# A mamba layer with a routed mixture of experts on one core: first fold, tag loads, an early turn and a reshared combine

## What is computed

```python
# layer 1: mamba-like block, then an MLP (256 -> 1024 -> 256)
xn = layernorm(x) * w + b
g = xn @ gate_w + gate_b                      # halves gate, gate_gate through silu
u  = (xn * gate) @ state_w + state_b
Bm = gate_gate @ state_w + state_b
delta = softplus(mean(xn @ state_w + state_b))
y = scan(h = exp(-delta) * h + delta * Bm * u)
x = x + y @ out_w + out_b
x = x + gelu(layernorm(x) @ mlp_w1 + mlp_b1) @ mlp_w2 + mlp_b2
# layer 2: 8 experts, 2 chosen for each token
xn = layernorm(x) * ln_gamma + ln_beta
abel_out = gelu(xn @ abel_w + abel_b)
topw, topi = top_k(xn @ moe_gate_w + moe_gate_b, 2); w = softmax(topw)
eo[e] = gelu(xn @ ew1[e] + eb1[e]) @ ew2[e] + eb2[e]
moe_out = sum_e w[e] * eo[e];  moe_out = moe_out @ expm(gens[i])  for i in 0..2
gate = sigmoid(concat(abel_out, moe_out) @ gc_w + gc_b)
out = layernorm(x + residual + abel_out * (1 - gate) + moe_out * gate)
```

## Time and profile before

| what | value |
|---|---|
| time of three runs | 727.7, 729.74, 888.66 us, median 729.74 |
| the profiled execution | 730.6 us, of which 728.7 us from the first to the last instruction |
| PE / PEld / DVE / ACT / POOL busy | 87% / 65% / 81% / 64% / 34% |
| mean granted TensorE clock | 0.945 |
| DMA | 99.21 MB, mean 136 GB/s |

### The profile page before, as it was taken

How to read it: one execution, slowest core, us unless ns; L and a number is a source line. 1 busy time by engine, 2 the same in 40 slices (tenths; PEclk the granted TensorE clock), 3 DMA queues, 4 the chain that set the end, 5 groups by cost and what they waited for, 6 DMA issues and landing times. The chain is left out here.

```text
span 728.7 us, 16183 instructions
## 1 busy us (share of the span) xinstructions
PE 632.1 (87%) x4525; PEld 473.6 (65%) x4526; DVE 587.5 (81%) x1535; ACT 462.9 (64%) x876; POOL 248.2 (34%) x295
## 2 busy tenths in 40 slices
PE   6899999999999999999979995889999999996000
PEld 5667557575665857566556884678888888885000
DVE  4989768899998999899798875577788878784693
ACT  4346573956658494765757344667777777774197
POOL 2111020125436081633516540133434344444042
PEclk9999999999999999999998997999999999999555
DMA  5643223165644537356725824465666655310974
GB/s 146 197 148 58 87 42 80 55 127 193 117 152 103 135 109 157 119 103 236 171 87 176 275 99 109 112 162 148 160 166 160 164 132 126 77 58 4 303 246 144
DMA packets 124502, 99.21 MB, mean 136 GB/s; under 512 B 60432, under 2 KB 114587, under 8 KB 124316
## 3 DMA queue, kind: packets, MB, share of 16 engines
q1 hardware_dynamic: 108028, 68.82, 33.4%
q0 software_dynamic: 16416, 29.67, 17.4%
HBM read 62.42 MB, written 33.68 MB: 132 GB/s over the span
## 5 line engine op out<-in xcount | busy, mean ns | idle before, releaser
L1920 POOL DMA_INDIRECT scratch_ys<-ye,place x78 | 86.9, 1114 | 149.4 <-ACT ye L1964 109.5
L79 PE MATMUL up<-shared,words 128*128 128x256 bf16 x936 | 112.3, 278 | 13.0 <-PEq L1738 7.8
L79 PE MATMUL bank<-words 128*128 128x512 bf16 (+1 forms) x576 | 109.4, 343 | 3.8 <-DVE logits L1077 3.2
L79 PE MATMUL down<-words,shared 128*128 x936 | 110.5, 274 | 1.8 <-DVE yb L2051 1.1
L79 PEld LDWEIGHTS up<-shared,words 128*128 x936 | 93.1, 100 | 26.9 <-issue 14.3
L79 PEld LDWEIGHTS down<-words,shared 128*128 128x128 bf16 x936 | 90.8, 98 | 15.9 <-issue 3.6
L79 PE MATMUL bank<-xn_s,mlp_w 128*128 128x512 bf16 x384 | 89.5, 387 | 2.2 <-DVE xn_s L798 2.2
L79 PEld LDWEIGHTS bank<-words 128*128 128x128 bf16 x576 | 55.4, 98 | 50.4 <-issue 6.6
L79 PE MATMUL bank<-mlp_w,shared 128*128 128x256 bf16 x768 | 86.4, 273 | 0.0
L510 POOL DMA_INDIRECT scratch_zs<-rows,pos x64 | 71.0, 1109 | 37.2 <-DVE pos L1127 18.5
L79 PEld LDWEIGHTS bank<-mlp_w,shared 128*128 128x128 bf16 x768 | 74.9, 98 | 10.6 <-issue 0.4
(11 more groups left out here) (247 smaller groups left out, 1151.4 us busy)
## 6 DMA issues: line engine op xcount, KB each, us to landing
fetched<-scratch_zs SPq DMA_DIRECT2D x156, 64.0 KB
words<-scratch_ys SPq DMA_DIRECT2D x16, 514.0 KB, 8.5
scratch_abel<-staged SPq DMA_DIRECT2D x8, 514.0 KB, 3.7
abel_all<-scratch_abel SPq DMA_DIRECT2D x8, 514.0 KB
x_in<-in_x SPq DMA_DIRECT2D x8, 512.0 KB, 5.6
words<-in_out_b_row SPq DMA_DIRECT2D x8, 512.0 KB, 4.1
fetched<-in_mlp_b_row SPq DMA_DIRECT2D x8, 512.0 KB, 3.5
words<-in_x POOLq DMA_DIRECT2D x8, 512.0 KB, 7.9
```

The lines of the kernel that those rows point to most:

```text
L79: last = nc.tensor.matmul(dst, lhs(a, k), rhs(b, k), start=start and n == 0, stop=stop and n == total - 1)
L1920: nc.gpsimd.indirect_dma_start(out=ys_dram[:, :], out_offset=bass.IndirectOffsetOnAxis(ap=place[:, k, s:s + 1], axis=0), in_=ye[:, k % 2, ...
```

## The change

Line numbers below are those of the diff; none of the arithmetic that is wanted changes, but for the order of the additions' engines.

1. **First fold and ring.** The ring's order becomes ew1 0 to 3, ew2t 0, ew1 4 to 7, ew2t 1 to 7. `fold(0)` runs around `turn2(LAST)`, its heads and tails in that region; all later folds, heads and tails move up by one expert, and one `w1_tails` moves from before the last routing but one to behind it. `fold_bank` and the waits of chunks 0 to 7 follow.
2. **Nine products** `ident` x `turnmat` that nobody reads, behind the last fold (`BUSY_BEFORE_TILES`).
3. **Tile 1 turned early**, in phase 1 instead of in `body(0)`; ScalarE's table load moves to phase 1 too; all `w2_heads` and `w2_tails` come ahead of the turn of tile 0.
4. **Tag loads one by one**: each `load(q)` issues the tags of its own tile; tiles 0 and 1 follow in `load(2)` and `load(3)`. `load_branch` comes behind a group's four loads.
5. **Half steps at the bias**: `down` signals each of its two halves, `biased` waits for each.
6. **The combine** is shared out anew (last part of the diff): TensorE adds the two rows of a token (identity times `got`, two float32 products of 257 columns for each token tile, into PSUM) for half of batches 1 and 2 and for all of 3 to 7; VectorE then only subtracts; batch 0 is loaded and added in halves; 30 unread products (`KEPT_BUSY`) run ahead of the sums; of the four finishing operations ScalarE keeps two, GpSimd does two in batches 0 to 5 and VectorE two in batches 6 and 7. The orders on VectorE and ScalarE follow.

```diff
+        RAW_ORDER = [("ew1", e) for e in range(RAW - 1)] + [("ew2t", 0)] \
+            + [("ew1", e) for e in range(RAW - 1, NE)] + [("ew2t", e) for e in range(1, NE)]
...
-            return bank[(0, 1, 5, 4)[m % 4] if m < 4 * FC else (6, 7, 0, 1, 5, 4)[(m - 4 * FC) % 6]]
+            return bank[(2, 0, 1, 4)[m] if m < 4 else (0, 1, 5, 4)[m % 4] if m < 4 * FC else (6, 7, 0, 1, 5, 4)[(m - 4 * FC) % 6]]
...
             norm2_split(LAST)
+            w2_tails((0,))
             norm3_rows(LAST - 1)
...
             z4_tails(LAST - 1)
-            w1_tails((4,))
+            w2_tails((1, 2, 3))
             gelu_tail(LAST, 4)
             gelu_tail(LAST, 5)
-            w1_tails((5,))
+            w1_tails((4,))
...
-            w1_tails((6,))
+            w1_tails((5, 6))
             branch_sum(LAST, LAST % 2, 0)
             w1_tails((7,))
             branch_sum(LAST, LAST % 2, 1)
             norm3(LAST)
-            w2_tails(range(0, FC))
+            w2_tails(range(FC, 2 * FC))
...
-            dve.wait_ge(zs_in[0], 64)
-            turn_rows(nc, xt[:, 0], xb[:, 0], xT_done)
-            w2_tails(range(NE * FC - 3, NE * FC - 1))
+            for n in range(FETCHED):
+                dve.wait_ge(zs_in[n], 64)
+                turn_rows(nc, xt[:, n], xb[:, n], xT_done)
...
+            fold(0, (0, 1))
             turn2(LAST)
+            fold(0, (2, 3))
             mlp_up(LAST, range(0, 2))
+            pe.wait_ge(w2_tail, 1)
             turn4(LAST - 1, BATCHES)
             mlp_up(LAST, range(2, HC))
+            pe.wait_ge(w2_tail, FC)
             branch(LAST - 1, BATCHES)
             mlp_down(LAST, (0,))
             ranks(LAST - 1)
             mlp_down(LAST, (1,))
-            fold(0)
             fold(1)
+            fold(2)
             turn4(LAST, BATCHES + 1)
-            fold(2, (0, 1))
+            fold(3, (0, 1))
             branch(LAST, BATCHES + 1)
...
+            pe.wait_ge(w2_tail, 6 * FC)
+            for n in range(BUSY_BEFORE_TILES):
+                nc.tensor.matmul(bank[2 + n % 2][:, 0:DG], ident[:, :], turnmat[:, n % KC], start=True, stop=True)
...
 +                else:
+                    dve.wait_ge(sum_r, summed(b))
+                    nc.vector.tensor_tensor(diff[:, b % 2], banks[:, b % 2 * TT:b % 2 * TT + TT, 0:DG], abel[:, b],
+                                            ALU.subtract).then_inc(diff_r, 1)
...
+            def finished(b):
+                pool.wait_ge(shift_r, b + 1)
+                for n in pool_tiles(b):
+                    nc.gpsimd.tensor_scalar(got[:, b, 0, n, 0:D], mix[:, b % MIX, n], rs[:, b % 2, n:n + 1],
+                                            shift[:, b % 2, n:n + 1], ALU.mult, ALU.add).then_inc(res_p, 1)
...
             differ(0)
+            mixed(0)
             differ(1)
-            mixed(0)
-            for b in range(BATCHES):
-                if b + 2 < BATCHES:
-                    differ(b + 2)
-                if b > 0:
+            variances(0)
+            mixed(1)
+            shifts(0)
+            finished(0)
+            differ(2)
+            for b in range(1, BATCHES):
+                if b > 1:
                     shifts(b - 1)
+                    finished(b - 1)
                 if b + 1 < BATCHES:
                     mixed(b + 1)
                 variances(b)
+                if b + 2 < BATCHES:
+                    differ(b + 2)
...
+            def sums(b):
+                if b > 2:
+                    pe.wait_ge(diff_r, differences(b - 2))
+                pe.wait_ge(got_in[b], 32)
+                for n in range(added_by_vector(b), TT):
+                    nc.tensor.matmul(banks[:, b % 2 * TT + n, 0:DG], ident[:, :], got[:, b, 0, n], start=True, stop=False)
+                    nc.tensor.matmul(banks[:, b % 2 * TT + n, 0:DG], ident[:, :], got[:, b, 1, n], start=False, stop=True)\
+                        .then_inc(sum_r, 1)
...
+            pe.wait_ge(yb_r, ST * QT)
+            for n in range(KEPT_BUSY):
+                nc.tensor.matmul(banks[:, n % TT, 0:DG], ident[:, :], turnmat[:, n % KC], start=True, stop=True)
+            for b in range(1, BATCHES):
+                sums(b)
```

More of the change, by code:

```diff
@@ L1807, in experts @@
         ye = sb("ye", [P, 2, ST, DG])
-        up_bank = [[pb(f"up{i}{j}", [P, 2, SLOT]) for j in range(2)] for i in range(2)]
-        down_bank = [pb(f"down{n}", [P, 512]) for n in range(ST)]
+        banks = pb("banks", [P, 8, 512])
+        up_bank = [[banks[:, 2 * i + j].rearrange("p (c n) -> p c n", c=2) for j in range(2)] for i in range(2)]
+        down_bank = [banks[:, 4 + n] for n in range(ST)]
         zs_in = kept["added"][5:9]
@@ L1830, in experts, with added_by_vector, summed, differences @@
         block = ctx.enter_context(nc.Block())
+        def added_by_vector(b):
+            return TT if b == 0 else TT // 2 if b < 3 else 0
+        def summed(b):
+            return sum(TT - added_by_vector(k) for k in range(b + 1))
+        def differences(b):
+            return sum(2 if k < 3 else 1 for k in range(b + 1))
+        def act_tiles(b):
+            return range(TT // 2)
+        def pool_tiles(b):
+            return range(TT // 2, TT if b < BATCHES - 2 else TT // 2)
+        def vector_tiles(b):
+            return range(pool_tiles(b).stop, TT)
+        def finished_by_act(b):
+            return sum(len(act_tiles(k)) for k in range(b + 1))
+        def finished_by_vector(b):
+            return sum(len(vector_tiles(k)) for k in range(b + 1))
+        def finished_by_pool(b):
+            return sum(len(pool_tiles(k)) for k in range(b + 1))
+        def wait_finished(eng, b):
+            wait(eng, res_r, finished_by_act(b))
+            wait(eng, res_p, finished_by_pool(b))
+            wait(eng, res_v, finished_by_vector(b))
         def rows_of(dram, b):
@@ L1992, in finished @@
                 act.wait_ge(shift_r, b + 1)
-                for n in range(TT):
+                for n in act_tiles(b):
                     nc.scalar.activation(got[:, b, 0, n, 0:D], mix[:, b % MIX, n], ACT.Identity,
```

179 lines of the change are left out of this document (108 added, 71 removed).

## The result

The changed kernel takes 717.59 us (median of four executions, 717.39 to 717.64) against 729.15 for the kernel before. The ratio, which leaves out the one slow execution of the kernel before (888.66 us), is 0.985, 95% interval 0.983 to 0.987. That is 1.5% faster, within the 2% that I called the edge, and 3.0 us above my forecast of 714.6. Against the profiled execution the forecast's sum was 15.1 us; the spans differ by 728.7 - 715.6 = 13.1.

The account below looks back on a forecast made before the run. TensorE bounds the steady tiles, so gains lie in phase 1's end, first tiles and combine: 1.1 + 7.9 + 0.9 + 3.3 + 3.9 - 2.0 = 15.1 us off 730.6, less 0.9, 714.6 us; own range 711 to 718, eight in ten 709.5 to 722.5.

Parts of the forecast that it names:

- First fold and ring: End of phase 1: folding in TensorE's waits keeps its clock up; 2.65 us less 1.53 for four tails, 1.1 won.
- Half steps at the bias: Around the last down products: two waits each lose their first half, about 0.45 us, 0.9 us won; steady tiles unchanged.
- The combine: After the tiles: 3.3 us won in four VectorE steps, 3.9 in ScalarE's finish, 2.0 lost to GpSimd's disturbance.
- the edge: Two per cent faster, 715.1 us, about what a measurement can tell from no change; the forecast of 714.6 lies there.
- First tiles: Start of the tile phase: fewer tag loads ahead of fetches, up(4) 6.1 us earlier plus 1.84 from the clock, 7.9 won.
- Tile 1's early turn: nothing: First tiles: takes a 0.7 us instruction off VectorE where it waits anyway; no gain or cost.
- the nine products: nothing: Ahead of the tiles: 4.1 us of unread products run while TensorE would idle, so they cost nothing.
- Ahead of batch 3 I count nothing: Combine's first batches: first rows 1.5 us earlier by halving the first load, given back by the new order; net nothing.
- GpSimd's duration: Combine: one GpSimd finishing instruction over 256 columns takes 0.26 to 0.57 us.
- a sign of being wrong: Combine: a GpSimd tile of over 1 us was one of three observations said to make the prediction wrong.
- The median is 0.9 lower: Whole kernel: profiled execution 730.6 us, median 729.74, so 0.9 was taken off 715.5 to give 714.6 us.
- Cold TensorE: Rival, chance 0.06: TensorE runs the combine at 1.2 GHz, its sums are on the path, 744.4 us.

Follow-up runs that it names:

- the load order alone: Kernel before with only the new order of tag and branch loads in the tiles: 723.61 us, against 728.02 for the kernel before.
- the old order: Changed kernel with the kernel before's order of tag and branch loads in the tiles put back: 720.40 us, against 717.46 for the changed kernel.

## Why the prediction was right or wrong

The mechanisms held in the main, and the result is inside the range; the time came out 3.0 us over the forecast, two of them from the sum and one from the step from the profiled execution to the median. Read by medians instead, the forecast's 15.1 us of gain are 10.6 (728.02 and 717.46 in one group). Undone one at a time, load order, combine, phase 1 and half steps cost 2.9 + 3.8 + 1.7 + 0.6 = 9.0 of these; with the 4.4 of the load order alone it is 10.5.

- **First fold and ring: right.** 1.1 forecast, 1.0 at the fetch, 1.1 between two rows of one trace. The up products take 2.54 us for 11 records at full clock, where 2.65 was forecast for 12. That only 1.1 of the time won there reaches the fetch is what the forecast derived from VectorE's four tails; no run took the tails away.
- **First tiles: right in the trace, too large for the median.** up(4) starts 477.88 - 470.14 = 7.7 us earlier, 6.7 of them behind the first fetch (6.1 forecast). But the trace of before was one of the slowest executions, and by the second trace of the old order (221.90 against 226.12 us) at least part of its excess sits in just these waits: the edit alone brings 7.2 us by traces and 4.4 by medians, undone 2.9. Against medians this is the term that was most too large.
- **"Tile 1's early turn: nothing", "the nine products: nothing".** The turn is not nothing: it puts a wait for a transfer ahead of a barrier for all engines, and 0.3 us or more are lost. The products bring 0.3 to 1.6 us by the traces, if anything.
- **Half steps at the bias: right** (0.9 forecast, 1.0 by the traces of before and after: 0.4 ahead of the last down products, 0.6 behind).
- **The combine: the sum right by luck, its parts not.** 5.2 forecast, 5.0 measured. The step without GpSimd is 3.74 us, exactly the forecast's, and its tiles add 0.24, not 0.4, in four steps, not five. In the trace the four steps win 4 x (4.57 - 3.98) = 2.4, not 1.7. "Ahead of batch 3 I count nothing" was wrong: from the first load to the end of batch 3's subtraction (686.46 - 665.47) it takes 21.0 us, where the kernel before took 19.4. By then VectorE has mixed three batches and not two, since the new order puts a batch's mixing ahead of the next difference. The first rows do come earlier (3.6 us behind the first load, not 5.4), but that does not make it good. The mixing that now stands ahead is missing at the end, where from the last difference to the last finish 12.2 us become 7.9 (4.3, not 3.9, won).
- **GpSimd's duration: too low.** 0.26 to 0.57 us forecast from a memset and a select, 0.56 to 1.05 measured. The longest is above the 1 us that I had named as a sign of being wrong; but even so GpSimd stayed off the path: power and two tiles are 2.5 us of a 3.98 us step. The Trainium skill's rule (SBUF — State Buffer, "Who interferes with whom"), that the second to issue of such a pair blocks until the first is through, could cost VectorE up to 1.5 us a batch, the length of both tiles. The measured 0.24 is far below it. Two of VectorE's instructions a batch are prolonged by 0.12 us each: a mixing that starts at 698.83, while GpSimd's first tile runs from 698.61 to about 699.17, would have to stand still for 0.34 us by the rule. GpSimd's second tile, issued behind that mixing, takes 0.96 us where the first takes 0.56. For VectorE as the second the trace does not agree with the rule, as far as GpSimd's spans can be read that finely, and the measurement decides.
- **The end: the step that failed.** The forecast has no term for it: I kept the stretch behind the last finish at its old length. It grew by 1.3 us, in a wait of SyncE for TensorE's sequencer (0.9 to 2.2). This is the larger part of the two microseconds by which 13.1 falls short of 15.1; the rest is 0.5 in the tiles and 0.2 in the combine. Which of the new combine's instructions prolongs it is open: no run took TensorE's sums away and kept the rest.
- **"The median is 0.9 lower": wrong for the changed kernel.** 715.5 was the sum; I took off what the profiled run of before stood above its median. The changed kernel's profiled execution (717.39) is at its median. That the excess belonged to waits that the change removes is the likely reason.
- **Cold TensorE: refuted.** It assumed that a clock that has fallen stays down. Without the 30 products it falls, and costs 1.0 us by the medians.
- **The range.** My own range for the forecast, 711 to 718, is too narrow by its own ends: contention of 1 us a batch is 3.0 us over the forecast, and the first fold at 0 another 1.1, so 718.7. The result lies inside either way.

## What to carry to other kernels

Before sizing a gain at a place where an engine waits for transfers, see how the profiled execution stands to its median: a slow sample can have its excess in just those waits, as seems to be so here, and then it must not be taken off the changed kernel's time again. Before comparing two traces, find a row ahead of every edit and measure from there: here the start alone moves all that follows by up to 1.6 us. A wait placed ahead of a barrier for all engines is paid by all of them, even where its own engine has time. When work moves to an engine that was idle at the end of the program, look at what the end itself waits for.

## What the runs showed of the hardware

- Two groups of 24 float32 products at the program's start take 5.47 to 6.99 and 6.81 to 8.46 us in fourteen traces with the same code there, 13.2 to 14.8 together. The scan at 57 us follows the end of the second by 28.8 us in each, so all later work is shifted by up to 1.6 us. The second group starts behind 4.2 us in which TensorE stands idle, and for a part of it the granted clock is 0.50. It is back at 1.00 by 26 us in the changed kernel, but from 26 to 28 us still 0.64 in the one without the nine products. In the first group the granted clock is 1.00 throughout in both; what prolongs it is open.
- TensorE's clock rose from 0.50 to 0.95 and 1.00 in the combine of the kernel without the 30 products once the sums left no gaps, and cost about a microsecond in all.
- Beside GpSimd instructions that read 256 columns per partition, two of four VectorE instructions with two SBUF inputs take 0.60 instead of 0.48 us, and one of 514 columns 0.93 instead of 0.69. The power (4 columns) takes 1.01 us beside a VectorE instruction with one input in PSUM, and took 1.98 beside one with both in SBUF.
- At the end of the program SyncE waits 2.1 or 2.2 us for TensorE's sequencer in the eleven traces in which TensorE works in the combine, and 0.9 in the three in which it does not. Why is open.
